# The deep stage's norms on VectorE and ScalarE, its probabilities multiplied on GpSimd, and a new order of the steps

## The chip, the cores and the metric

The kernel runs as one launch on one core of a Trainium2 chip. A core has TensorE (PE, matmuls into PSUM), VectorE (DVE), ScalarE (ACT), GpSimd (POOL) and SyncE (SP, which issues DMAs). Each engine runs its own instructions in order; semaphores tie them together. The metric is the device time of one execution in microseconds. Before the change it is 4638.97 us, the median of three runs (4630.0 to 4643.03).

## The reference

Twelve sublayers are applied in turn to x, four sequences of 512 tokens with 128 channels, each as `x = x + 0.5 * f(layernorm(x))` or without the half: mixture of experts, attentions, channel mixes, SwiGLU, a forget attention, a time mix, and twice the stage of this case, `_L3_ffn_ref`, called "deep":

```python
for i in range(DEPTH):          # 6 layers
    x = attn_layer(shift_tokens(x), Wqkv[i], q_scale[i], k_scale[i], Wo[i]) + x
    x = ffn_layer(shift_tokens(x), ln_g[i], ln_b[i], W1[i], b1[i], W2[i], b2[i]) + x
```

`attn_layer` makes q, k and v of 16 heads of 64, divides each head's q and k by max(norm, 1e-12), multiplies by learned scales and by rotary tables, and attends in windows of 32 tokens to the own and the previous window, with a softmax; its output goes through Wo. `ffn_layer` is a layer norm with gain and offset, a product to twice 341 channels, a times the exact Gelu of the gate, and a product back to 128. All of it is float32.

## The kernel before

x and z lie in SBUF as 128 channels by 2048 tokens, cut into NB = 4 blocks of T = 512. The deep stage works on units: one layer of one block. There are 6 x 4 = 24 units, each of 4 tiles of 128 tokens, so ALL = 96 tiles; the stage runs twice. Each engine's program walks over the steps `s` (`deep_pe`, `deep_act`, `deep_dve`, `deep_pool`), and the order in a step is written out by hand. In step s four tiles are in flight: q and k of tile s are made, tile s-1 is turned, tile s-2 gets its scores and softmax, and tile s-3 its mix with V. `n` is the step's unit and `t` the step in it. The end of unit n-2, its layer norm and feed-forward product, is spread over the four steps (`ending`), and so is Wo of unit n-1 (`begun`).

The work on one tile, with the lines of the profile:

- TensorE multiplies to q, then to k, two matmuls of 512 columns each into PSUM banks 2 and 3 (`qk_pe`, line 1297). ScalarE squares them (1466). VectorE multiplies by the sine and cosine tables (1584, 1588) and sums the squares for each head (1595).
- GpSimd adds the two rotary parts (1703), clamps the sums of squares (1708), raises them to -1/2 (1710) and multiplies q or k with the result (1716). TensorE turns them with eight transposes (1314), ScalarE evicts (1472).
- Scores: eight bf16 matmuls write the mask, 64 small matmuls of 64 rows add q by k (1260, 1266), into banks 0 and 1. V: four products (1328), evicted by ScalarE (1499), moved by SyncE's DMAs.
- Softmax: VectorE takes the maximum (1552), subtracts it (1559), ScalarE does Exp (1476), VectorE sums, inverts (1565, 1567) and multiplies the probabilities (1572). TensorE turns them (1280), ScalarE evicts (1483).
- Mix: 64 small matmuls (1347) into banks 0 and 1 again, evicted as o (1490). Wo: three and five products (1361, 1366).

The end of a unit: mean (1374), centring (1611), squares (1503), variance (1379, 1615), the root as a power on GpSimd (1721), spread over the partitions (1385), scaling (1621), affine (1510), gates (1396), Gelu (1515), a-products (1406), hidden (1630), down product (1412), sum (1636). The banks 4 and 5 hold by turns v, turned q, turned k and turned probabilities, banks 6 and 7 the end of the unit.

Of the kernel before, what the change touches and what calls it, by code (L numbers as in the profile page):

```python
# [19 lines left out]
P = 128  # L20
# [25 lines left out]
def program(nc, d, out, sublayers):  # L46
    with ExitStack() as ctx:
# [25 lines left out]
        minus_half = sb("minus_half", [P, LHEADS])  # L73
# [1079 lines left out]
        def time_dve(dve, u, q, pads):  # L1153
# [19 lines left out]
            for b in range(NB):  # L1173
# [14 lines left out]
                if b >= 1:  # L1188
# [7 lines left out]
                  "deep_sq_summed deep_clamped deep_inv_ready deep_rope_parts deep_summed deep_roped deep_turned deep_turn_kept "  # L1196
# [14 lines left out]
        qT = new(PAIRS, T)  # L1211
# [4 lines left out]
        roped = new(2 * LHEADS, LD)  # L1216
# [5 lines left out]
        h_sum, h_inv = [new(2 * LHEADS) for _ in range(2)], [new(2 * LHEADS) for _ in range(2)]  # L1222
# [26 lines left out]
        def scores_pe(pe, c, j):  # L1249
# [12 lines left out]
            for pair in range(PAIRS):  # L1262
                for jj in range(WPT):
                    for r in range(2):
                        r64, wi = slice(64 * r, 64 * r + 64), WPT * t + jj
                        last = nc.tensor.matmul(bank(r)[32 * jj:32 * jj + 32, pair * 64:pair * 64 + 64],  # L1266
                                                qT[r64, pair, wi * WIN:(wi + 1) * WIN],
                                                kT[r64, pair, wi * WIN:(wi + 2) * WIN], start=False,
                                                stop=(pair == PAIRS - 1), skip_group_check=True)
            last.then_inc(de.deep_scores_ready, 1)  # L1270
# [30 lines left out]
        def turn_pe(pe, c, a, half):  # L1301
            i = c * ALL + a
            pe.wait_ge(de.deep_roped, 2 * i + half + 1)
            if half == 1 and a >= 1:
                pe.wait_ge(de.deep_v_kept, i)
            elif half == 1:
                pe.wait_ge(de.deep_turn_kept, 2 * i + 1)
            elif a >= 2:
                pe.wait_ge(de.deep_probs_kept, i - 1)
            elif a == 1:  # L1310
                pe.wait_ge(de.deep_turn_kept, 2 * i)
            for m in range(PAIRS):
                h = LHEADS * half + 2 * m
                last = nc.tensor.matmul(turns[:, m * P:(m + 1) * P], roped[:, h:h + 2, :], w.ident[:, :], start=True, stop=True,  # L1314
# [3 lines left out]
        def value_pe(pe, c, a):  # L1318
            i, unit_, t = c * ALL + a, a // TILES, a % TILES
            if a + 1 < ALL:  # L1320
                pe.wait_ge(de.deep_turn_kept, 2 * i + 3)
            else:
                pe.wait_ge(de.deep_probs_kept, i)
# [8 lines left out]
        def mix_pe(pe, c, j):  # L1332
# [7 lines left out]
            for pair in range(0, PAIRS, 2):  # L1340
# [9 lines left out]
            last.then_inc(de.deep_pv_done, 1)  # L1350
# [64 lines left out]
        def deep_pe(pe, c):  # L1415
            for s in range(LAST + 1):
                n, t = s // TILES, s % TILES
                ending, begun = 0 <= n - 2 < UNITS, 0 <= n - 1 < UNITS
                if s < ALL:
                    qk_pe(pe, c, s, 0)  # L1420
                if t == 0 and ending:
                    mean_pe(pe, c, n - 2)
                if t == 1 and ending:
                    gate_pe(pe, c, n - 2, 0)
                if 0 <= s - 1 < ALL:
                    turn_pe(pe, c, s - 1, 0)
                if 0 <= s - 2 < ALL:
                    scores_pe(pe, c, s - 2)
                if t == 2 and ending:
                    a_pe(pe, c, n - 2, 2)  # L1430
# [636 lines left out]
```

## Time and profile before

| | |
|---|---|
| median of three runs | 4638.97 us |
| the profiled execution's own time | 4619.88 us |
| its span, first to last instruction | 4618.2 us |
| mean granted clock | 0.964 of full speed |
| busy: TensorE, GpSimd, VectorE, ScalarE | 91%, 67%, 74%, 48% of the span |
| deep stages, from the span's start | about 1067 to 2802 and 2887 to 4612 us |

The trace is one execution. "Busy" is the union of an engine's instructions; matmuls are pipelined and their ends are modelled. A group row gives engine, operation, output and input, count, then busy time, mean ns of one, and the idle time ahead of them with what ended it. PE is the matmul, PEld the weight load. A float32 matmul appears as two records, a transpose as one. "Issue" is time in which the engine waited for nothing that the profile shows.

### The profile page before, as it was taken

What the parts mean: (1) busy time and instruction counts of PE and PEld (TensorE: products, weight loads), DVE (VectorE), ACT (ScalarE), POOL (GpSimd) and SP (SyncE); (2) the same over time, 40 slices, a digit from 0 to 9 for tenths busy, and PEclk for the clock granted to TensorE, in tenths of its full rate; (3) what the DMA queues carried; (4) which work ended last, traced back from release to release, by engine and by line L of the source; (5) the groups of instructions that cost most, each with busy time, mean ns of one, the idle gap of its engine ahead of it and who ended that gap; (6) DMA issues with size and microseconds to landing.
All of it is one profiled execution on the core that took longest, in us unless ns stands there. A gap on an engine that the chain in (4) does not pass through costs nothing.

```text
span 4618.2 us, 148108 instructions
## 1 busy us (share of the span) xinstructions
PE 4211.8 (91%) x66796; PEld 2446.3 (53%) x66796; DVE 3412.0 (74%) x3977; ACT 2202.5 (48%) x2637; POOL 3088.0 (67%) x1726
## 2 busy tenths in 40 slices
PE   7997999867999999999999996799999999999998
PEld 4543433434555555555555553455555555565554
DVE  6567666466777877778778766687788888888885
ACT  1451355323555555555555551355555555555553
POOL 0110000017998898988988960988988988989984
PEclk8998899978999999999999997899999999999999
DMA  2000000001111111111121111111211212121111
GB/s 81 1 2 1 1 1 1 1 0 42 29 32 53 32 31 54 31 53 33 28 56 32 29 32 48 23 32 29 56 29 32 56 29 56 27 57 32 29 32 32
DMA packets 78609, 144.87 MB, mean 31 GB/s; under 512 B 18648, under 2 KB 24992, under 8 KB 76448
## 3 DMA queue, kind: packets, MB, share of 16 engines
q1 hardware_dynamic: 77984, 135.39, 11.5%
q8 instruction: 532, 8.72, 0.8%
q14 instruction: 93, 0.76, 0.1%
HBM read 39.91 MB, written 1.05 MB: 9 GB/s over the span
## 4 chain that ended last, share of the span: by engine, by line
PE 59%; POOL 22%; issue 9%; DVE 8%; ACT 1%; DMA 0%; SPq 0%; POOLq 0%; DVEq 0%
PE psum L1297 9%; POOL arena L1710 8%; POOL arena L1703 6%; POOL arena L1716 5%; PE psum L1314 5%; PE psum L1328 5%; PE psum L666 5%; PE psum L1366 4%; PE psum L1347 4%; PE psum L1266 4%; PE psum L1412 3%; PE psum L1361 3%; PE psum L698 3%; PE psum L720 3%; PE psum L1406 2%
## 5 line engine op out<-in xcount | busy, mean ns | idle before, releaser
L1710 POOL TENSOR_TENSOR arena<-arena,minus_half 128x16 f32<-128x16 f32 x384 | 1129.6, 2942 | 32.0
L1703 POOL TENSOR_TENSOR arena<-arena 128x1024 f32<-128x1024 f32 x384 | 909.2, 2368 | 12.3 <-DVE arena L1588 12.3
L1584 DVE TENSOR_TENSOR arena<-psum,arena 128x1024 f32<-128x1024 f32 x384 | 467.7, 1218 | 399.8 <-ACT arena L1466 399.8
L1716 POOL TENSOR_TENSOR arena<-arena 128x1024 f32<-128x1024 f32 x384 | 733.7, 1911 | 42.6
L1472 ACT ACTIVATE arena<-psum 128x1024 f32<-128x1024 f32 x384 | 392.2, 1021 | 297.5 <-PE psum L1314 297.2
L1466 ACT ACTIVATE arena<-psum 128x1024 f32<-128x1024 f32 x384 | 391.9, 1020 | 253.8 <-PE psum L1297 250.4
L1588 DVE TENSOR_TENSOR arena<-psum,arena 128x1024 f32<-128x1024 f32 x384 | 466.3, 1214 | 54.5 <-PE psum L1314 54.5
L1314 PEld LDWEIGHTS psum<-w_ident,arena 128*128 128x128 f32 x3072 | 354.7, 141 | 279.9 <-issue 151.5
L1499 ACT ACTIVATE arena<-psum 128x1024 f32<-128x1024 f32 x192 | 196.5, 1024 | 580.6 <-PE psum L1328 580.6
L1595 DVE TENSOR_REDUCE arena<-arena 128x16 f32<-128x1024 f32 x384 | 464.4, 1210 | 2.8
L1314 PE MATMUL psum<-w_ident,arena 128*128 128x128 f32 x3072 | 405.6, 275 | 46.3 <-POOL arena L1716 45.4
L1347 PE MATMUL psum<-arena 64*64 64x32 f32 x24576 | 407.2, 220 | 28.6 <-issue 28.5
L1297 PE MATMUL psum<-deep_wqkv,arena 128*128 128x512 f32 x768 | 390.9, 633 | 35.7 <-DVE arena L1588 27.8
L1347 PEld LDWEIGHTS psum<-arena 64*64 64x64 f32 x24576 | 381.8, 135 | 67.4 <-issue 67.3
L1297 PE MATMUL psum<-arena 128*128 128x512 f32 x768 | 372.2, 606 | 0.0
L1266 PE MATMUL psum<-arena 64*32 64x64 f32 x24576 | 296.2, 224 | 66.4 <-issue 66.0
L1266 PEld LDWEIGHTS psum<-arena 64*32 64x32 f32 x24576 | 282.1, 105 | 86.8 <-issue 76.6
L1035 POOL TENSOR_TENSOR arena<-arena 128x512 f32<-128x512 f32 x10 | 14.3, 1450 | 465.8 <-DVE arena L1016 451.7
L1708 POOL TENSOR_SCALAR arena<-arena 128x16 f32<-128x16 f32 x384 | 151.1, 393 | 246.1 <-DVE arena L1595 245.9
L1483 ACT ACTIVATE arena<-psum 128x1024 f32<-128x1024 f32 x192 | 195.6, 1019 | 242.9 <-PE psum L1280 236.8
L1572 DVE TENSOR_TENSOR arena<-arena 128x1024 f32<-128x1024 f32 x192 | 301.7, 1571 | 5.9
L666 PE MATMUL psum<-arena 32*128 32x512 f32 (+3 forms) x1024 | 302.6, 588 | 3.4 <-ACT arena L805 2.3
(264 smaller groups left out, 7277.6 us busy)
## 6 DMA issues: line engine op xcount, KB each, us to landing
arena<-arena SPq DMA_DIRECT2D x672, 128.0 KB, 2.3
deep_wqkv<-in_deep_wqkv SPq DMA_DIRECT2D x6, 1536.0 KB, 7.0
arena<-in_deep_wqkv SPq DMA_DIRECT2D x6, 1536.0 KB, 7.0
arena<-arena SPq DMA_DIRECT2D x96, 64.0 KB, 2.6
deep_wo<-in_deep_wo SPq DMA_DIRECT2D x6, 512.0 KB, 7.3
arena<-in_deep_wo SPq DMA_DIRECT2D x6, 512.0 KB, 7.4
deep_w<-in_deep_w SPq DMA_DIRECT2D x6, 341.0 KB, 7.5
arena<-in_deep_w SPq DMA_DIRECT2D x6, 341.0 KB, 7.4
```

The source lines that it names most:

```text
L666: nc.tensor.matmul(bank(v % SCORE_BANKS)[:, 0:keys], da_Q[r32, b * SETS + s, x_ * P:(x_ + 1) * P], keys_of(causal, b, s)[r32, 0:keys], sta ...
L1266: last = nc.tensor.matmul(bank(r)[32 * jj:32 * jj + 32, pair * 64:pair * 64 + 64], qT[r64, pair, wi * WIN:(wi + 1) * WIN], kT[r64, pair, w ...
L1297: last = nc.tensor.matmul(bank(2 + cc), xs[unit_ % 2][:, WIN + t * P:WIN + (t + 1) * P], wqkv[:, half * INNER + cc * 512:half * INNER + (c ...
L1314: last = nc.tensor.matmul(turns[:, m * P:(m + 1) * P], roped[:, h:h + 2, :], w.ident[:, :], start=True, stop=True, is_transpose=True)
L1347: last = nc.tensor.matmul(bank(odd)[64 * side:64 * side + 64, to:to + WIN], V[64 * r:64 * r + 64, WPT * t + jj, (pair + odd) * 64:(pair + ...
L1472: nc.scalar.activation(dst, turns.rearrange("p (c t) -> p c t", t=P), ACT.Copy).then_inc(de.deep_turn_kept, 1)
L1584: nc.vector.tensor_tensor(turned[:, hs, :].rearrange("p h (a e) -> p h a e", a=2), swapped, sin, ALU.mult).then_inc(de.deep_rope_parts, 1)
L1588: nc.vector.tensor_tensor(roped[:, hs, :], qk_half, under(tabs[:, 2 * half, t, :], shape), ALU.mult).then_inc(de.deep_rope_parts, 1)
L1595: nc.vector.tensor_reduce(h_sum[a % 2][:, hs], qk_sq[:, hs, :], AX.X, ALU.add).then_inc(de.deep_sq_summed, 1)
L1703: nc.gpsimd.tensor_tensor(roped[:, hs, :], roped[:, hs, :], turned[:, hs, :], ALU.add).then_inc(de.deep_summed, 1)
L1710: nc.gpsimd.tensor_tensor(h_inv[a % 2][:, hs], h_inv[a % 2][:, hs], minus_half[:, :], ALU.pow).then_inc(de.deep_inv_ready, 1)
L1716: nc.gpsimd.tensor_tensor(roped[:, hs, :], roped[:, hs, :], over(h_inv[a % 2][:, hs], [P, LHEADS, LD]), ALU.mult).then_inc(de.deep_roped, 1)
```

## The change

**Norms.** VectorE writes the sums of squares of a tile into the first of each pair of `h_pair`, whose second holds the floor 1e-24; a reduce by maximum over the pair is the clamp, a reciprocal over the 32 heads follows (`norms_dve`), and ScalarE takes the Sqrt in the next step (`norms_act`). GpSimd's clamps and powers (`rope_inv_pool`) are gone. GpSimd scales q and k a step later than before; `roped` has two buffers for it, `qT` two tiles instead of a whole block.

**Probabilities.** `divide_dve` becomes `divide_pool`, on GpSimd between the two rotary sums, ahead of the layer norm's root.

**Order.** Scores and mix are each cut into two halves of 64 small float32 products (in pairs of heads), with the value product or the turn of k between. On TensorE the scores go ahead of the turn of q. The mean moves from step 0 to the step 3 before; centring to the start of step 0. On ScalarE the affine step stands behind the Sqrt, and q's eviction behind Exp. The root's spread follows the turn of the probabilities, in transpose mode.

**Copies.** Four VectorE copies of a unit are written as reduces over one element.

```diff
-        minus_half = sb("minus_half", [P, LHEADS])
+        minus_half = sb("minus_half", [P, TILES])
+        h_pair = sb("h_pair", [P, 2 * LHEADS, 2])
...
-        def mix_pe(pe, c, j):
+        def mix_open_pe(pe, c, j):
...
+            mix_pe(j, 0)
+
+        def mix_close_pe(pe, c, j):
+            mix_pe(j, 1).then_inc(de.deep_pv_done, 1)
...
-                                        w.ident[:, :], start=True, stop=True)
+                                        w.ident[:, :], start=True, stop=True, is_transpose=True)
...
                 if s < ALL:
                     qk_pe(pe, c, s, 0)
+                if 0 <= s - 2 < ALL:
+                    scores_open_pe(pe, c, s - 2)
+                    value_pe(pe, c, s - 2)
+                    scores_close_pe(pe, c, s - 2)
                 if t == 0 and ending:
-                    mean_pe(pe, c, n - 2)
+                    var_pe(pe, c, n - 2)
                 if t == 1 and ending:
                     gate_pe(pe, c, n - 2, 0)
+                if t == 2 and ending:
+                    a_pe(pe, c, n - 2, 2)
+                if t == 3 and begun:
+                    wo_rest_pe(pe, c, n - 1)
                 if 0 <= s - 1 < ALL:
                     turn_pe(pe, c, s - 1, 0)
...
                 if s < ALL:
                     qk_pe(pe, c, s, 1)
-                if t == 3 and begun:
-                    wo_rest_pe(pe, c, n - 1)
+                if 0 <= s - 3 < ALL:
+                    mix_open_pe(pe, c, s - 3)
                 if t == 1 and ending:
                     gate_pe(pe, c, n - 2, 1)
                 if 0 <= s - 1 < ALL:
                     turn_pe(pe, c, s - 1, 1)
+                if t == 3 and begun:
+                    mean_pe(pe, c, n - 1)
                 if 0 <= s - 3 < ALL:
-                    mix_pe(pe, c, s - 3)
+                    mix_close_pe(pe, c, s - 3)
...
+        def norms_act(act, c, a):
+            i = c * ALL + a
+            act.wait_ge(de.deep_sq_inv, i + 1)
+            if a >= 2:
+                act.wait_ge(de.deep_roped, 2 * i - 2)
+            nc.scalar.activation(h_inv[a % 2], h_rcp, ACT.Sqrt).then_inc(de.deep_inv_ready, 1)
...
-                if t == 1 and ending:
-                    affine_act(act, c, n - 2)
                 if 0 <= s - 3 < ALL:
                     probs_act(act, c, s - 3)
                 if s < ALL:
                     square_act(act, c, s, 0)
                 if 0 <= s - 1 < ALL:
-                    turn_act(act, c, s - 1, 0)
+                    norms_act(act, c, s - 1)
+                if t == 1 and ending:
+                    affine_act(act, c, n - 2)
                 if t == 0 and ending:
                     ln_square_act(act, c, n - 2)
                 if 0 <= s - 2 < ALL:
                     value_act(act, c, s - 2)
                     exp_act(act, c, s - 2)
+                if 0 <= s - 1 < ALL:
+                    turn_act(act, c, s - 1, 0)
...
+        def norms_dve(dve, c, a):
+            i = c * ALL + a
+            dve.wait_ge(de.deep_sq_summed, 2 * i + 2)
+            nc.vector.tensor_reduce(h_low, h_pair[:, :, :], AX.X, ALU.max).then_inc(de.deep_clamped, 1)
+            dve.wait_ge(de.deep_clamped, i + 1)
+            if a >= 1:
+                dve.wait_ge(de.deep_inv_ready, i)
+            nc.vector.reciprocal(h_rcp, h_low).then_inc(de.deep_sq_inv, 1)
...
-            nc.vector.tensor_copy(xf[0:64, :], zu[0:64, :]).then_inc(de.deep_ffn_shifted, 1)
+            nc.vector.tensor_reduce(xf[0:64, :], single(zu[0:64, :]), AX.X, ALU.max).then_inc(de.deep_ffn_shifted, 1)
...
+        def divide_pool(pool, c, j):
+            i = c * ALL + j
+            pool.wait_ge(de.deep_row_inv, i + 1)
+            nc.gpsimd.tensor_tensor(flat[j % 2], flat[j % 2], over(row_inv, R), ALU.mult).then_inc(de.deep_probs_ready, 1)
...
+                if 0 <= s - 1 < ALL:
+                    rope_scale_pool(pool, c, s - 1, 0)
+                    rope_scale_pool(pool, c, s - 1, 1)
                 if s < ALL:
                     rope_sum_pool(pool, c, s, 0)
+                if 0 <= s - 2 < ALL:
+                    divide_pool(pool, c, s - 2)
                 if t == 0 and 0 <= n - 2 < UNITS:
                     rstd_pool(pool, c, n - 2)
                 if s < ALL:
-                    rope_inv_pool(pool, c, s, 0)
-                    rope_scale_pool(pool, c, s, 0)
-                    rope_inv_pool(pool, c, s, 1)
                     rope_sum_pool(pool, c, s, 1)
-                    rope_scale_pool(pool, c, s, 1)
```

VectorE's order in a step becomes: centring (t = 0), parts of q, maximum and subtraction, sums of q's squares, row sum and reciprocal, the sum of Wo (t = 3), parts of k, sums of k's squares, norms, then scaling (t = 0), the shift of the next unit's input (t = 1, before at t = 2), hidden.

## Rows read from the trace of the kernel before

**Rows 1.** Windows, one in each deep stage: busy us of each engine, clock, DMA.
```profile
core 0: us, PE busy (x) PEld busy (x) DVE busy (x) ACT busy (x) POOL busy (x), PEclk, DMA share, GB/s
1200.00:2700.00 1500.00, 1414.53 (x27106) 866.76 (x27106) 1186.77 (x1198) 802.22 (x838) 1346.82 (x728) 1.00 0.15 38
3000.00:4500.00 1500.00, 1431.40 (x27344) 874.63 (x27345) 1214.29 (x1206) 808.05 (x840) 1354.67 (x731) 1.00 0.15 38
```

**Rows 2.** Timeline of VectorE, the last instruction of two units: start, us.
```profile
1246.53 0.74 DVE L1636 SCALAR_TENSOR_TENSOR z<-psum,deep_vec,z 128x512 f32<-128x512 f32 x1
...
2649.61 0.74 DVE L1636 SCALAR_TENSOR_TENSOR z<-psum,arena,z 128x512 f32<-128x512 f32 x1
```

**Rows 3.** TensorE's waits from 1067 to 4612: us in total, times, longest.
```profile
PE psum L1266 <- issue: 66.0, 67, 1.6
PE psum L1314 <- POOL arena L1716: 45.4, 77, 2.1
PE psum L1385 <- POOL rstd L1721: 36.4, 46, 1.9
PE psum L1347 <- issue: 28.5, 37, 1.6
```

**Rows 4.** Chain of waits inside one unit, pieces in order: start, us, what.
```profile
2001.67 1.72 PE psum L1297 x4
2003.39 0.87 PE psum L1314 x8
2004.27 0.34 PE psum L1260 x8
2004.60 1.28 PE psum L1266 x85
...
2011.58 2.00 PE psum L1347 x128
...
2022.74 1.16 PE psum L1266 x78
2023.90 1.10 issue
...
2025.34 1.89 PE psum L1328 x8
2027.22 1.92 PE psum L1297 x4
2029.14 4.29 PE psum L1366 x10
```

**Rows 5.** Groups by line of the whole span: busy us, mean ns, idle before.
```profile
L1710 POOL TENSOR_TENSOR arena<-arena,minus_half 128x16 f32<-128x16 f32 x384 | 1129.6, 2942 | 32.0
L1703 POOL TENSOR_TENSOR arena<-arena 128x1024 f32<-128x1024 f32 x384 | 909.2, 2368 | 12.3 <-DVE arena L1588 12.3
L1716 POOL TENSOR_TENSOR arena<-arena 128x1024 f32<-128x1024 f32 x384 | 733.7, 1911 | 42.6
L1708 POOL TENSOR_SCALAR arena<-arena 128x16 f32<-128x16 f32 x384 | 151.1, 393 | 246.1 <-DVE arena L1595 245.9
L1721 POOL TENSOR_TENSOR rstd<-arena,minus_half 128x4 f32<-128x4 f32 x48 | 92.2, 1920 | 74.1 <-DVE arena L1615 74.1
L1572 DVE TENSOR_TENSOR arena<-arena 128x1024 f32<-128x1024 f32 x192 | 301.7, 1571 | 5.9
L1559 DVE TENSOR_TENSOR arena<-psum,arena 128x1024 f32<-128x1024 f32 x192 | 234.5, 1221 | 5.1
L1499 ACT ACTIVATE arena<-psum 128x1024 f32<-128x1024 f32 x192 | 196.5, 1024 | 580.6 <-PE psum L1328 580.6
```

**Rows 6.** Timeline of ScalarE where Sqrt is followed by Exp, in the time sublayer.
```profile
2813.07 0.27 ACT L193 ACTIVATE all_std<-psum,eps 128x16 f32<-128x16 f32 x1 [2.64 <-PE psum L172]
2813.36 1.28 ACT L1144 ACT_TABLE_LOAD   x1
2819.87 0.60 ACT L1144 ACTIVATE arena<-psum 128x512 f32<-128x512 f32 x1 [5.22 <-PE psum L1136]
```

More of the change, by code:

```diff
@@ L1210, in program @@
         tabs = new(4, TILES, LD)
-        qT = new(PAIRS, T)
+        qT = [new(PAIRS, P) for _ in range(2)]
         kT = new(PAIRS, WIN + T)
@@ L1215, in program @@
         turned = new(2 * LHEADS, LD)
-        roped = new(2 * LHEADS, LD)
+        roped = [new(2 * LHEADS, LD) for _ in range(2)]
         probs = [new(PAIRS, 2, 2 * WIN) for _ in range(2)]
@@ L1221, in program @@
         xs = [new(WIN + T) for _ in range(2)]
-        h_sum, h_inv = [new(2 * LHEADS) for _ in range(2)], [new(2 * LHEADS) for _ in range(2)]
+        h_low, h_rcp = new(2 * LHEADS), new(2 * LHEADS)
+        h_inv = [new(2 * LHEADS) for _ in range(2)]
         row_max, row_sum, row_inv = (new(LHEADS) for _ in range(3))
@@ L1261, in scores_pe, with scores_close_pe @@
                                      stop=False, skip_group_check=True)
-            for pair in range(PAIRS):
+            scores_pe(j, 0)
+        def scores_close_pe(pe, c, j):
+            scores_pe(j, 1).then_inc(de.deep_scores_ready, 1)
+        def scores_pe(j, part):
+            t = j % TILES
+            for pair in range(PAIRS // 2 * part, PAIRS // 2 * (part + 1)):
                 for jj in range(WPT):
@@ L1303, in turn_pe @@
             pe.wait_ge(de.deep_roped, 2 * i + half + 1)
-            if half == 1 and a >= 1:
+            if half == 1:
+                pe.wait_ge(de.deep_turn_kept, 2 * i + 1)
+            elif a >= 1:
                 pe.wait_ge(de.deep_v_kept, i)
[L1306 to L1311, printed above, removed]
             for m in range(PAIRS):
                 h = LHEADS * half + 2 * m
-                last = nc.tensor.matmul(turns[:, m * P:(m + 1) * P], roped[:, h:h + 2, :], w.ident[:, :], start=True, stop=True,
+                last = nc.tensor.matmul(turns[:, m * P:(m + 1) * P], roped[a % 2][:, h:h + 2, :], w.ident[:, :], start=True, stop=True,
                                         is_transpose=True)
@@ L1339, in mix_pe @@
             apart(pe)
-            for pair in range(0, PAIRS, 2):
+            mix_pe(j, 0)
+        def mix_close_pe(pe, c, j):
+            mix_pe(j, 1).then_inc(de.deep_pv_done, 1)
+        def mix_pe(j, part):
+            t = j % TILES
+            for pair in range(PAIRS // 2 * part, PAIRS // 2 * (part + 1), 2):
                 for jj in range(WPT):
@@ L1349, in mix_pe @@
                                                     probsT[64 * r:64 * r + 64, half, col:col + WIN], start=True, stop=True)
-            last.then_inc(de.deep_pv_done, 1)
+            return last
         WO_FIRST = 3
@@ L1449, in deep_pe @@
                     down_pe(pe, c, n - 2)
-                if t == 0 and ending:
-                    spread_pe(pe, c, n - 2)
                 if t == 2 and begun:
@@ L1455, in deep_pe @@
                     probs_turn_pe(pe, c, s - 2)
+                if t == 0 and ending:
+                    spread_pe(pe, c, n - 2)
                 if t == 1 and ending:
@@ L1654, in deep_dve @@
                 ending, begun = 0 <= n - 2 < UNITS, 0 <= n - 1 < UNITS
+                if t == 0 and ending:
+                    centre_dve(dve, c, n - 2)
+                if t == 2 and ending:
+                    hidden_dve(dve, c, n - 2, 1)
                 if t == 3 and ending:
@@ L1660, in deep_dve @@
                     max_dve(dve, c, s - 2)
[L1661 to L1663 removed]
                     less_max_dve(dve, c, s - 2)
+                if t == 0 and ending:
+                    var_dve(dve, c, n - 2)
                 if s < ALL:
@@ L1683, in deep_dve @@
                 if s < ALL:
+                    parts_dve(dve, c, s, 1)
                     squares_dve(dve, c, s, 1)
-                if t == 3 and begun:
-                    centre_dve(dve, c, n - 1)
+                    norms_dve(dve, c, s)
+                if t == 0 and ending:
+                    scale_dve(dve, c, n - 2)
+                if t == 1 and 2 <= n + 1 < UNITS:
+                    shift_dve(dve, c, n + 1)
                 if t == 1 and ending:
```

78 lines of the change are left out of this document (25 added, 53 removed).

## The prediction

> **What bounds the kernel now.** I read the busy time by windows first, then the clock of the units, then TensorE's waits, then the chain of waits inside one unit. [rows 1] are two stretches of 1500 us, one in each deep stage: TensorE is busy 1414.53 and 1431.40 us (94 and 95%), GpSimd 1346.82 and 1354.67 (90%), VectorE some 80%, ScalarE some 54%, and the granted clock is 1.00, its full level. So the engine to beat is TensorE; GpSimd is a near second. [rows 2] give the period: the instruction that ends a unit (four steps) starts at 1246.53 and, 20 units on, at 2649.61, so 70.15 us for one. TensorE's own time in it, by the mean of the two stretches, is 0.949 x 70.15 = 66.5; its idle time is 3.6.
>
> [rows 3] say what that idle time is. Over both deep stages TensorE waits 66.0 + 28.5 us for "issue", inside the bursts of the scores (line 1266) and of the mix (line 1347), and 45.4 + 36.4 for GpSimd, ahead of the turned q and k (1314) and of the spread root (1385). Over 44 steady units: 94.5 / 44 = 2.1 us of issue in a unit, 81.8 / 44 = 1.9 of GpSimd (a little of it in the first and last units, so that the two give more than 3.6). The reader is to see in [rows 4] how an issue gap looks: the burst of 128 pairs of a weight load and a small matmul runs 1.28 us; the next one breaks off after 78 records for 1.10 us, with no engine to blame. Bursts are the fastest readers of instructions in the stream, so I take the gap for TensorE's instruction stream running dry.
>
> **The change, part by part.** Time zero below is the end of the first qk product of a step.
>
> *GpSimd.* A step had two sums (2368 ns), two scalings (1911), two powers (2942) and two clamps (393) [rows 5]: 15.2 us. The powers and clamps go, the multiplication of the probabilities comes: 128x1024 with a broadcast operand as in the scaling, so 1.91 (at the other end 2.37, a sum's). New: 2 x 2.37 + 3 x 1.91 = 10.5 us, and a root of 1.92 in every fourth step. GpSimd stops being a bound by its sum; only its order can hurt.
>
> *VectorE.* It loses the multiplication (1571 ns, [rows 5]), 6.3 us a unit. It gains per step one reduce over 64 elements and a reciprocal of 32, each at most the 1.22 of a 1024-element instruction and nearer a fourth of it, say 0.6 together, 2.4 a unit; four copies become reduces of 512 elements, between nothing and 0.8 more each, I take 0.7 a unit. Net -3 us on an engine that is idle a fifth of the time: nothing by itself, and its cover is that idle time; were it gone it would still be a gain.
>
> *ScalarE.* A Sqrt of 128x32 a step, 0.27 as the one in [rows 6], and its table. Sqrt, Exp and Gelu alternate, so each step loads twice and one step in four a third time: 9 loads a unit instead of 2. A load is 1.28 us [rows 6]: 7 x 1.28 + 4 x 0.27 = +10 us a unit on an engine that is busy 0.535 x 70.15 = 37.5. The same group shows two things: the load starts 0.02 us after the instruction ahead of it, and it runs before the wait of its own activation, which starts only 5.2 us after the load's end. So a load falls into ScalarE's waiting time where there is any.
>
> *TensorE.* The spread of the root goes into transpose mode: 4 records instead of 8. A turn of eight transposes takes 0.87 [rows 4], so it saves 0.44 a unit. Scores and mix are cut in halves with value, turn or gates between. The half burst of 64 pairs is 0.64 us, then 1.89 us of value product, in which the stream can refill; the gap shown came after 78 records, past the point at which the burst is now cut. I take three quarters of the gaps away, 2.1 to 0.5 a unit; the ends are nothing and all. More changes between small and full tiles cost: a qk product takes 1.92 after the value product and 1.72 after a turn [rows 4], so 0.2 at most per change; three more such changes and one fewer in a step, 0.1 on the average: +0.5 a unit (ends 0 and 1.6).
>
> *What is late next.* With the norms on ScalarE a step later: square 1.02, load 1.28, Sqrt 0.27, some 0.1 of handing over, 2.7; the first scaling 1.91 ends at 4.65, so the turn of q can start at 4.7. TensorE arrives there after masks 0.34, scores 1.28, value 1.89 = 3.5 and the extra of the step. In step 0 that is the variance (eight small matmuls, estimated as 0.87), in 1 a gate and in 2 an a-product (0.86, half of 1.72): 4.4, so 0.3 of waiting in each. In step 3 it is the rest of Wo, 4.29: none. Exp: the value's eviction ends at 4.6, its load at 5.9, and the scores less their maximum are there at 6.0, 2.44 behind the end of value and scores at 3.5 (maximum and subtraction, 1.22 each by [rows 5]); so the load is just covered. Exp (1.05, as an eviction of that size) ends at 7.1, q's eviction at 8.2; TensorE has then done the turn (5.6), qk (7.3) and half the mix (8.3): it just fits. Row sum and reciprocal end at 8.8. GpSimd is at 2.7 + 2 x 1.91 + 2.37 = 8.9 and multiplies to 10.8 (its scaling starts as soon as the root is there). The turn of the probabilities is reached by TensorE at 10.2 in step 0 and later in the other three, which have gates, down product, or Wo between.
>
> In step 0 the root follows: 10.8 + 1.92 = 12.75. TensorE would be at the spread at 4.4 + 0.87 + 1.72 + 2.00 + 0.87 + 0.87 + 0.5 of changes = 11.2. So step 0 waits 1.55 (the 0.3 in it). The unit waits 1.55 + 0.3 + 0.3 = 2.15 for GpSimd, where it waited 1.5 (3.6 - 2.1) for all engines. SyncE's queue keeps its order; its moves of V are released by the value's eviction, which comes no later than before, and the mix that needs them is a step behind: nothing. The affine step now stands behind the Sqrt in ScalarE's order and ends at 3.5, ahead of the gate that needs it (3.5): nothing.
>
> Sum of a unit: 66.5 - 0.44 + 0.5 + 2.15 + 0.5 = 69.2, against 70.15: -0.95. With 44 steady units -42. At the head of a stage some five steps have no layer norm and no feed-forward product: there GpSimd's 15.2 is the bound and the new one is the turn of the probabilities, 10.8 + 0.87 + the next qk, 1.72, so 13.4 and some handing over; I put 4 us a stage, -8 (ends 0 and -20). The drain at the end is a chain that keeps its links: 0. Together -50. The profiled execution is 4619.88 us (span 4618.2 and 1.7 around it), 19 below the median of 4638.97; the difference is put on the median: **4589**, 1.1% faster.
>
> **The rivals.**
>
> *All cover holds.* The small waits of 0.3 and the 1.55 fall in gaps or are absorbed because nothing waits behind them: a unit of 67, 3.1 x 44 = 136 less, so some 4505. For it: the walk takes the later end of each link. Against: the root's chain is strictly serial on one queue.
>
> *The gaps stay.* If the stream runs dry for another reason than the density of the burst, 1.6 a unit come back, less some 0.3 that fall into waits: +57, 4646, within the measurement. For it: by [rows 3] only 67 of 192 score bursts break at all, so density alone does not make a gap. Against: the two lines with bursts hold all of it that matters.
>
> *Slower: ScalarE's order.* In step 1 ScalarE has probabilities, two squares, value, two turns and output (7 x 1.02, [rows 5]), Exp 1.05, three Gelus (2.0), affine 0.8, Sqrt 0.27 and three loads (3.9): 15.2 us of a step of some 16.6. It decides if its waits in order (now 580.6 / 192 = 3.0 us a step before the value alone, [rows 5]) can't be packed into the 1.4 that are left: then step 1 takes 15.2 + 3.0 + 1.0 for its other waits = 19.2, and the other steps 0.5 more, 2.6 + 1.5 = 4.1 a unit, +180: 4769. For it: two thirds busy and in strict order, each eviction holding the same pair of banks. Against: the walk above finds the waits where the loads are.
>
> *Slower: a switch of tables costs twice its load*, because the engine has to fall empty. Another 1.28 in front of Sqrt makes q's turn late by as much in three steps: +3.8 a unit, +169: 4758. [rows 6] speak against it: 0.02 us between the Sqrt and the load. The Trainium skill (ScalarE: Activation LUTs, What ACT_TABLE_LOAD costs) gives 1283 ns for the load and 1380 ns for a drain, 2.66 us a switch, and in Table sets: the hidden batching unit it advises to batch by set, which this change does the opposite of. By its figure the estimate would be 1.38 x 3 a unit, 4.1 x 44 = 182, some 4771. The trace agrees on the load and shows no drain.
>
> **How the numbers follow.** A measurement of this kernel can tell about 0.3% (14 us) from no change. Chances: forecast (4550 to 4622) 0.45, all cover holds 0.17, gaps stay 0.15, ScalarE's order 0.17, double switch 0.03, the change does nothing that matters 0.03. Faster: 0.45 + 0.17 + 0.04 of the third = 0.66. Within: 0.08 of the third, the last and a little of the fourth, 0.13. Slower: 0.21. The range goes from the covered case to the first part of ScalarE's: 4500 to 4680. The likeliest case alone spans 4550 to 4622, by its bounds on gaps and changes.
>
> **What would show it.** TensorE's waits for "issue" at scores and mix fall to a quarter. Its wait at the spread is about 1.2 us a unit, and the turn of q waits 0.3 in three steps of four. ScalarE shows some 430 loads of 1.28 us, busy near 69% in the deep stages. GpSimd falls to about 66% there. A unit takes 69.2. It would be wrong if ScalarE became the releaser of TensorE's long waits, if the GpSimd multiplication took far from 1.9 us, or if the issue gaps stayed at 2 us a unit.

## The result, and the profile after

The changed kernel takes 4494.47 us (median of four runs, 4482.29 to 4501.22), the kernel before 4634.49 beside it: ratio 0.9694, 95% interval 0.9675 to 0.9714, so 140 us less, where 50 were predicted. The profiled execution has a span of 4487.9 us, 130.3 less than before.

The page's first part, busy time by engine:

```profile
PE 4237.0 (94%) x66604; PEld 2403.9 (54%) x66604; DVE 3256.5 (73%) x4169; ACT 2676.0 (60%) x3161; POOL 2128.2 (47%) x1151
```

Windows of the changed kernel, one in each deep stage, as [rows 1]:

```profile
core 0: us, PE busy (x) PEld busy (x) DVE busy (x) ACT busy (x) POOL busy (x), PEclk, DMA share, GB/s
1200.00:2600.00 1400.00, 1394.55 (x26238) 823.07 (x26236) 1096.72 (x1250) 985.51 (x1040) 892.99 (x457) 1.00 0.16 40
2900.00:4300.00 1400.00, 1391.90 (x26371) 825.04 (x26370) 1098.08 (x1252) 986.60 (x1040) 897.40 (x459) 1.00 0.16 40
```

TensorE is busy 99.5% of the two windows, where it had 94 to 95; GpSimd fell from 90% to 64, ScalarE rose from 54 to 70. The ends of two units, as [rows 2]:

```profile
1232.84 0.75 DVE L1669 SCALAR_TENSOR_TENSOR z<-psum,deep_vec,z 128x512 f32<-128x512 f32 x1
...
2577.54 0.75 DVE L1669 SCALAR_TENSOR_TENSOR z<-psum,arena,z 128x512 f32<-128x512 f32 x1
```

A unit takes (2577.54 - 1232.84) / 20 = 67.24 us instead of 70.15. TensorE's waits over both deep stages, as [rows 3] (the window 1067 to 4480; line 1320 is the turn of q and k, 1290 that of the probabilities, 1397 the spread, 1276 and 1359 scores and mix):

```profile
PE psum L1320 <- POOL arena L1739: 15.1, 11, 3.3
PE psum L1290 <- POOL arena L1745: 12.1, 51, 1.5
PE psum L1397 <- POOL rstd L1749: 2.7, 2, 1.3
...
PE psum L1276 <- issue: 0.2, 1, 0.2
```

The 94.5 us of issue are 0.2, the 81.8 us of waiting for GpSimd are 29.9, most of it in the first steps of the stages. The groups of the moved work, as [rows 5]:

```profile
L1739 POOL TENSOR_TENSOR arena<-arena 128x1024 f32<-128x1024 f32 x384 | 722.3, 1902 | 881.8 <-ACT arena L1487 881.8
L1745 POOL TENSOR_TENSOR arena<-arena 128x1024 f32<-128x1024 f32 x192 | 365.3, 1903 | 66.9 <-DVE arena L1592 58.4
L1749 POOL TENSOR_TENSOR rstd<-arena,minus_half 128x4 f32<-128x4 f32 x48 | 48.8, 1016 | 47.5 <-DVE arena L1648 47.5
L1487 ACT ACT_TABLE_LOAD x188 | 241.2, 1283 | 3.3
L1497 ACT ACT_TABLE_LOAD x190 | 243.8, 1283 | 3.3
L1620 DVE TENSOR_REDUCE arena<-h_pair 128x32 f32<-128x64 f32 x192 | 42.2, 220 | 6.7
L1624 DVE RECIPROCAL arena<-arena 128x32 f32<-128x32 f32 x192 | 67.8, 353 | 6.9 <-DVE arena L1620 0.4
```

The multiplication takes 1.90 on GpSimd, the root 1.02 instead of 1.92. ScalarE and GpSimd in a step 0, on the timeline; the qk product ends at 1994.94:

```profile
1994.98 1.03 ACT L1480 ACTIVATE arena<-psum 128x1024 f32<-128x1024 f32 x1 [0.70 <-PE psum L1307]
1996.02 1.28 ACT L1487 ACT_TABLE_LOAD   x1
1997.31 0.23 ACT L1487 ACTIVATE arena<-arena 128x32 f32<-128x32 f32 x1
1997.45 0.62 ACT L1524 ACTIVATE xc_sq<-xc 128x512 f32<-128x512 f32 x1
1997.97 1.00 ACT L1520 ACTIVATE arena<-psum 128x1024 f32<-128x1024 f32 x1
1998.99 1.28 ACT L1497 ACT_TABLE_LOAD   x1
2001.17 1.06 ACT L1497 ACTIVATE arena<-arena 128x1024 f32<-128x1024 f32 x1 [0.89 <-DVE arena L1582]
```
```profile
1997.68 3.76 POOL L1739 TENSOR_TENSOR arena<-arena 128x1024 f32<-128x1024 f32 x2 [3.61 <-ACT arena L1487]
2001.40 2.37 POOL L1733 TENSOR_TENSOR arena<-arena 128x1024 f32<-128x1024 f32 x1
2003.85 1.90 POOL L1745 TENSOR_TENSOR arena<-arena 128x1024 f32<-128x1024 f32 x1
2005.71 1.01 POOL L1749 TENSOR_TENSOR rstd<-arena,minus_half 128x4 f32<-128x4 f32 x1
```

Put the zero at 1994.94: the Sqrt ends at 2.6 (walked: 2.7), GpSimd's multiplication at 10.8 (10.8), the root at 11.8 (12.75). The loads lie in waiting time: the Exp still waits 0.89 for the subtraction behind its load. In the chain of waits of that step TensorE comes to the turn of the probabilities almost with GpSimd:

```profile
1994.94 0.34 PE psum L1262 x8
1995.28 0.66 PE psum L1276 x49
1995.94 1.89 PE psum L1332 x8
1997.83 0.80 PE psum L1276 x53
...
2005.80 1.09 PE psum L1290 x8
2006.90 0.53 PE psum L1397 x4
```

### The profile page after: what moved, and what is told of

The parts are those of the page before. It is cut to its first block, busy times and chain, and to the rows that moved or that the text cites. A ratio compares the mean times of both kernels' runs of the same rounds, so it can differ in the third digit from the quotient of the medians.

```text
span 4487.9 us, 148433 instructions
## 1 busy us (share of the span) xinstructions
PE 4237.0 (94%) x66604; PEld 2403.9 (54%) x66604; DVE 3256.5 (73%) x4169; ACT 2676.0 (60%) x3161; POOL 2128.2 (47%) x1151
## 4 chain that ended last, share of the span: by engine, by line
PE 77%; POOL 8%; issue 7%; DVE 6%; ACT 2%; DMA 0%; SPq 0%; POOLq 0%; DVEq 0%; ACTq 0%
PE psum L1307 13%; PE psum L1359 7%; PE psum L1332 6%; PE psum L1320 6%; PE psum L1276 5%; PE psum L667 5%; PE psum L1378 5%; PE psum L1290 4%; POOL arena L1739 3%; PE psum L1408 3%; PE psum L1424 3%; PE psum L1418 3%; PE psum L1373 3%; PE psum L699 3%; PE psum L721 3%
## 5 line engine op out<-in xcount | busy, mean ns | idle before, releaser
L1739 POOL TENSOR_TENSOR arena<-arena 128x1024 f32<-128x1024 f32 x384 | 722.3, 1902 | 881.8 <-ACT arena L1487 881.8
L1733 POOL TENSOR_TENSOR arena<-arena 128x1024 f32<-128x1024 f32 x384 | 907.5, 2363 | 245.0 <-DVE arena L1608 245.0
L1480 ACT ACTIVATE arena<-psum 128x1024 f32<-128x1024 f32 x384 | 392.4, 1022 | 288.2 <-PE psum L1307 288.2
L1493 ACT ACTIVATE arena<-psum 128x1024 f32<-128x1024 f32 x384 | 390.8, 1018 | 194.6 <-PE psum L1320 194.6
L1615 DVE TENSOR_REDUCE h_pair<-arena 128x16 f32<-128x1024 f32 x384 | 464.2, 1209 | 0.0
L1359 PE MATMUL psum<-arena 64*64 64x32 f32 x24576 | 437.9, 221 | 5.2 <-DVE arena L1582 5.1
L1320 PEld LDWEIGHTS psum<-w_ident,arena 128*128 128x128 f32 x3072 | 338.2, 141 | 162.0 <-POOL arena L1739 94.6
L1745 POOL TENSOR_TENSOR arena<-arena 128x1024 f32<-128x1024 f32 x192 | 365.3, 1903 | 66.9 <-DVE arena L1592 58.4
L1504 ACT ACTIVATE arena<-psum 128x1024 f32<-128x1024 f32 x192 | 196.7, 1024 | 257.9 <-PE psum L1290 251.6
L1276 PE MATMUL psum<-arena 64*32 64x64 f32 x24576 | 327.2, 223 | 0.3 <-issue 0.2
L667 PE MATMUL psum<-arena 32*128 32x512 f32 (+3 forms) x1024 | 303.6, 590 | 3.4 <-ACT arena L806 2.3
L1497 ACT ACTIVATE arena<-arena 128x1024 f32<-128x1024 f32 x192 | 202.9, 1057 | 173.8 <-DVE arena L1582 173.8
L699 PE MATMUL psum<-arena 32*128 32x512 f32 (+3 forms) x1024 | 293.3, 558 | 1.8 <-ACT arena L831 1.8
L1575 DVE TENSOR_REDUCE arena<-psum 128x16 f32<-128x1024 f32 x192 | 235.2, 1225 | 61.1 <-PE psum L1276 61.1
L831 ACT ACTIVATE arena<-psum 128x512 f32<-128x512 f32 (+3 forms) x344 | 161.0, 514 | 170.8 <-PE psum L699 169.4
```

Of the source, the lines that this page charges most:

```text
L667: nc.tensor.matmul(bank(v % SCORE_BANKS)[:, 0:keys], da_Q[r32, b * SETS + s, x_ * P:(x_ + 1) * P], keys_of(causal, b, s)[r32, 0:keys], sta ...
L699: nc.tensor.matmul(bank(key_at[m])[:, q0:T], kk[r32, kt * P:(kt + 1) * P], da_Q[r32, b * SETS + s, q0:T], start=True, stop=True).then_inc( ...
L1320: last = nc.tensor.matmul(turns[:, m * P:(m + 1) * P], roped[a % 2][:, h:h + 2, :], w.ident[:, :], start=True, stop=True, is_transpose=True)
L1359: last = nc.tensor.matmul(bank(odd)[64 * side:64 * side + 64, to:to + WIN], V[64 * r:64 * r + 64, WPT * t + jj, (pair + odd) * 64:(pair + ...
L1480: nc.scalar.activation(qk_sq[:, HALVES[half], :], qk_half, ACT.Square).then_inc(de.deep_qk_squared, 1)
L1615: nc.vector.tensor_reduce(h_pair[:, hs, 0], qk_sq[:, hs, :], AX.X, ALU.add).then_inc(de.deep_sq_summed, 1)
```

## The experiments

All are timed against the kernel before on their own chip; ratios to it in brackets. Waits are of the window 1250 to 2450, some 17 units of the first deep stage. A half is 32 float32 products, which are 64 records in the profile (the section on the change calls it 64 products).

**Halves alone, on the kernel before.**

```diff
-                    scores_pe(pe, c, s - 2)
...
-                    value_pe(pe, c, s - 2)
+                    scores_open_pe(pe, c, s - 2)
+                    value_pe(pe, c, s - 2)
+                    scores_close_pe(pe, c, s - 2)
...
+                if 0 <= s - 3 < ALL:
+                    mix_open_pe(pe, c, s - 3)
                 if 0 <= s - 1 < ALL:
                     turn_pe(pe, c, s - 1, 1)
                 if 0 <= s - 3 < ALL:
-                    mix_pe(pe, c, s - 3)
+                    mix_close_pe(pe, c, s - 3)
```


> The kernel before with the one edit that scores and mix are cut in halves of 64 pairs, the value product between the halves of the scores and the turn of k between those of the mix; norms, GpSimd and all other orders as before. Theory A (the issue gaps come from dense bursts that read the instruction stream dry): TensorE's waits for issue at scores and mix fall from 94.5 us to under 10, and the time by 50 to 80 us, to 4555 to 4585. Theory B (GpSimd's 15 us a step is a bound just behind TensorE, and the gaps only fill its time): the issue waits fall too, but TensorE's waits for GpSimd grow from 82 us by about as much, and the time stays within 20 us of 4634. Theory C (the gaps have another cause, such as the data transfers): issue stays near 95 us and so does the time.

Measured 4701.87 us (1.0147, 1.0126 to 1.0168): 66 slower. Its waits:

```profile
PE psum L1399 <- POOL rstd L1737: 22.7, 17, 1.3
PE psum L1321 <- POOL arena L1732: 11.6, 17, 0.7
PE psum L1410 <- ACT arena L1531: 9.8, 17, 0.6
PE psum L1361 <- DVE arena L1575: 9.1, 16, 0.6
PE psum L1335 <- ACT arena L1488: 4.6, 29, 0.2
```

No issue is left in the window (in the second stage 5.1 us, at the mix), so the halves end nearly all gaps; no theory had the rest. In the old order the value product needs q evicted, now sits inside the scores and holds their second half up; maximum, subtraction, root and mix follow later. These waits only take the place of the gaps, though: over 20 units from 1318.76 to 2745.90 TensorE is idle 3.9 us a unit, as before. What is added is its own busy time, 67.50 us a unit instead of 66.12 (12.4 us more at the mix and 10.3 at the scores in the 20), which I put down to more changes between small and full tiles.

**GpSimd relieved, on the kernel before.**

```diff
-            nc.gpsimd.tensor_tensor(h_inv[a % 2][:, hs], h_inv[a % 2][:, hs], minus_half[:, :], ALU.pow)
+            nc.gpsimd.tensor_tensor(h_inv[a % 2][:, hs], h_inv[a % 2][:, hs], minus_half[:, :], ALU.mult)
```

> The kernel before with GpSimd's power of 128x16 replaced by a product of the same shape, so that GpSimd is relieved of most of 2 x 2.94 us a step (the inverse root of the norms is left out); all orders as before. Theory A and B both: TensorE's waits for GpSimd (82 us) go. Theory A: the issue gaps of 94.5 us stay, and the time falls by 60 to 80 us, to about 4565. Theory B: with GpSimd out of the way the gaps are all that is left, and the time falls by less than 50 us, since what waited for GpSimd now meets the gaps.

Measured 4516.76 (0.9742, 0.9728 to 0.9757): 119 less, more than expected. GpSimd's waits are down to the spread, and in the first stage the gaps stay:

```profile
PE psum L1266 <- issue: 36.2, 35, 3.0
PE psum L1385 <- POOL rstd L1721: 4.4, 18, 0.3
PE psum L1347 <- issue: 3.7, 8, 0.7
```

In the second stage they nearly go, with the same code, whole bursts and full clock. These are 20 units of each stage, and the waits of the second 20:

```profile
1310.67:2679.78 1369.11, 1319.54 (x25358) 810.81 (x25355) 1109.56 (x1120) 747.76 (x780) 803.29 (x678) 1.00 0.16 39
3098.34:4425.70 1327.36, 1311.74 (x25361) 809.22 (x25361) 1110.57 (x1119) 749.34 (x780) 803.50 (x678) 1.00 0.16 41
```
```profile
PE psum L1266 <- issue: 5.3, 15, 0.5
PE psum L1347 <- issue: 5.0, 13, 1.0
```

So the gaps at the bursts are 2.2 us a unit in one stage and 0.5 in the other, and dense bursts alone do not make them; what differs between the stages is open. The unit there takes 66.37 us, less than the changed kernel's 67.24.

**Both of them.** The two edits together.

> Both edits of the two kernels above at once on the kernel before (the inverse root of the norms is left out). If the two causes are all of the change, this comes to the changed kernel's 4494 us within 20, with TensorE busy 98% or more of the deep stages. If the new order of scores ahead of the turn of q, or the probabilities on GpSimd, bring something of their own, it stays 40 us or more above. If the causes add up, its gain is the sum of the two single gains within 15 us; if each hides the other (theory B), it is more than the sum by 30 us or more.

Measured 4684.72 (1.0101, 1.0081 to 1.0121). With GpSimd out of the way the halves cost 168 us in the old order. The gains do not add; in this order the halves are a loss.

**Whole bursts, on the changed kernel.**

```diff
-                    value_pe(pe, c, s - 2)
                     scores_close_pe(pe, c, s - 2)
+                    value_pe(pe, c, s - 2)
...
-                if 0 <= s - 3 < ALL:
-                    mix_open_pe(pe, c, s - 3)
...
                 if 0 <= s - 1 < ALL:
                     turn_pe(pe, c, s - 1, 1)
...
+                    mix_open_pe(pe, c, s - 3)
                     mix_close_pe(pe, c, s - 3)
```


> The changed kernel with scores and mix as whole bursts again (value behind the scores, turn of k ahead of the mix), the rest as changed. Theory A: the issue gaps come back with 80 to 100 us, and the time rises by 60 to 90 us, to about 4570. If the gaps were made by anything but the density of the bursts, issue stays near 0 and the time rises by less than 15 us; it may even fall by up to 25 us, if the changes between tile sizes cost what was predicted (0.5 us a unit).

Measured 4621.41 (0.9976, 0.9959 to 0.9993): 127 slower than the changed kernel, and close to the kernel before. The trace is of an execution of 4637.41 us. Its window and waits:

```profile
1250.00:2450.00 1200.00, 1134.91 (x21515) 677.50 (x21512) 898.75 (x1028) 811.95 (x856) 736.64 (x380) 0.99 0.16 40
```
```profile
PE psum L1359 <- issue: 24.9, 26, 4.2
PE psum L1320 <- ACT arena L1492: 16.7, 34, 0.5
PE psum L1276 <- issue: 12.6, 19, 1.1
PE psum L1320 <- ACT arena L1519: 5.6, 26, 0.2
```

Issue comes back at 37.5 / 17.1 = 2.2 us a unit, but 1.3 more are waits of the turns for ScalarE: for the evictions of q (line 1492) and of v (1519). The value product stands later, and behind it hang its eviction, the table load, Exp and q's eviction. The halves pay twice.

**Only the scores whole; only the mix whole.** The two parts of that edit, one at a time.

> The changed kernel with the scores as one burst ahead of the value product; the mix stays in halves. Theory D (the halves pay twice: the instruction stream keeps up, and the value product comes 0.7 us earlier for ScalarE's chain of value, table load, Exp, q's eviction, turn of k): issue gaps of 0.7 to 1.2 us a unit come back at the scores alone, none at the mix, and TensorE waits some 0.5 us a unit for ScalarE ahead of the turn of k; 4530 to 4560. Theory A alone (only the stream): issue gaps as said, no wait for ScalarE; 4525 to 4540.

> The changed kernel with the mix as one burst behind the turn of k; the scores stay in halves. Theory D: issue gaps come back at the mix alone, 0.7 to 1.5 us a unit; and the turn of k, now 1.0 us earlier in the order, waits for q's eviction some 0.5 us in two of four steps; 4540 to 4580. Theory A alone: 4525 to 4545 and no wait for ScalarE. If neither gap nor wait shows, the mix's halves were worth nothing and the run is 10 to 25 us faster than the changed kernel, for two fewer changes of tile size a step.

Measured 4489.74 (0.9696, 0.9670 to 0.9722) for the scores: equal to the changed kernel, against both theories. Issue is 5.1 us in 18 units, the turns wait 8.8 for GpSimd and 1.9 for ScalarE, and TensorE's saved changes pay for that: its busy time is 66.36 us a unit instead of 66.97. The mix: 4560.95 (0.9849, 0.9824 to 0.9873), 66 slower:

```profile
PE psum L1320 <- ACT arena L1492: 29.0, 39, 0.8
PE psum L1359 <- issue: 6.9, 9, 1.1
PE psum L1276 <- issue: 2.6, 4, 1.2
```

So the mix's halves do the work, by covering q's eviction ahead of the turn of k (1.7 us a unit) more than by the gaps (0.6). With one burst whole the gaps are 0.3 to 0.6 us a unit and with both 2.2, and the costs, -5 and 66 us, add up to half of the 127: why is open.

**One more table load a step.**

```diff
+            nc.scalar.activation(sqrt_first[:, 2:3], eps[:, :], ACT.Sigmoid)
             nc.scalar.activation(h_inv[a % 2], h_rcp, ACT.Sqrt).then_inc(de.deep_inv_ready, 1)
```

> The changed kernel with one more table load a step: a Sigmoid on a scratch column ahead of the Sqrt, which loads its own table (1.28 us, and about 0.2 for the column). It stands for a switch that costs twice. If GpSimd's start is the tight link, as the prediction's walk has it (q's turn can start at 4.7, TensorE arrives at 4.4 to 4.6), the 1.5 us go onto three steps of four and onto the root in step 0: 4 to 5 us a unit, 180 to 220 us, 4680 to 4710. If ScalarE has slack there that the walk did not see, it is under 60 us.

Measured 4714.24 (1.0182, 1.0160 to 1.0204): 220 more than the changed kernel; a unit of the first stage takes 71.85 us, 4.6 more, as the walk's tight link says.

```profile
PE psum L1320 <- POOL arena L1740: 35.9, 50, 1.5
PE psum L1408 <- ACT xc L1532: 20.1, 17, 1.2
PE psum L1391 <- ACT xc_sq L1525: 17.2, 17, 1.0
```

A late Sqrt holds up q's turn, and the gate and the variance, which wait for the affine step and the squares behind it. That the loads which the change adds cost next to nothing is read from the changed kernel's small waits, and not from a run without them.

**GpSimd's powers back, as idle work.** `burn_pool` is a power of two scratch tiles.

```diff
                     rope_scale_pool(pool, c, s - 1, 0)
+                    burn_pool(pool)
                     rope_scale_pool(pool, c, s - 1, 1)
+                    burn_pool(pool)
```

> The changed kernel with GpSimd's two powers of 128x16 a step put back as work on a scratch tile, one behind each scaling; nothing uses them. GpSimd then has 10.5 + 5.9 = 16.4 us a step, near the step of 16.8. If GpSimd's relief is what makes the new order possible, the multiplication of the probabilities ends 5.9 us later and TensorE waits in every step: 150 to 400 us more. If the order alone makes the gain, it stays within 60 us of 4494.

Measured 5220.18 (1.1268, 1.1245 to 1.1292): 726 more, beyond the range. The turn of the probabilities waits 136.8 us in the window for GpSimd, and the granted clock is 0.93 there instead of 1.00. A unit of the first stage takes 82.09 us: of the 14.9 more, 11.1 are TensorE idle and 3.8 its own slower work. GpSimd is busy only 80% of it, so it is its place in the chain that costs, and not its sum.

**The spread without transpose mode; copies instead of reduces; the root ahead of the probabilities; the multiplication on VectorE.**

```diff
-                                        w.ident[:, :], start=True, stop=True, is_transpose=True)
+                                        w.ident[:, :], start=True, stop=True)
```
```diff
-            nc.vector.tensor_reduce(xf[0:64, :], single(zu[0:64, :]), AX.X, ALU.max).then_inc(de.deep_ffn_shifted, 1)
+            nc.vector.tensor_copy(xf[0:64, :], zu[0:64, :]).then_inc(de.deep_ffn_shifted, 1)
...
```
```diff
-                if 0 <= s - 2 < ALL:
-                    divide_pool(pool, c, s - 2)
                 if t == 0 and 0 <= n - 2 < UNITS:
                     rstd_pool(pool, c, n - 2)
+                if 0 <= s - 2 < ALL:
+                    divide_pool(pool, c, s - 2)
```
```diff
-                    divide_pool(pool, c, s - 2)
...
+                    divide_dve(dve, c, s - 2)
                 if t == 3 and begun:
                     attn_dve(dve, c, n - 1)
```

> The changed kernel with the root's spread as a plain float32 product (8 records instead of 4). By the prediction's term it costs 0.44 us a unit, 20 us. If TensorE is the only bound now (99.6% busy), all of it shows: 4505 to 4520. If step 0 still waits for GpSimd elsewhere, less than 10 us show.

> The changed kernel with the four reduces over one element a unit written as copies again. VectorE wins 4 x 0.2 us a unit and has slack, so nothing is won there. Theory: copies held GpSimd up (the clamp before took 393 ns in the mean and 250 in most), now GpSimd has slack too: within 15 us of 4494. Rival: a GpSimd instruction in the tight link behind the Sqrt is held up by copies, 0.3 to 1 us a unit: 15 to 45 us more.

> The changed kernel with the layer norm's root ahead of the multiplication of the probabilities in GpSimd's order in step 0. The turn of the probabilities stands ahead of the spread on TensorE and then waits for the root's length more. If the root takes 1.0 us as in the changed kernel: 1.0 us a unit, 40 to 50 us. The root took 1.92 in the kernel before, where it stood right behind a sum; here it does again. If its length goes by the instruction ahead of it, it is 1.9 to 2.0 again and the cost 80 to 95 us.

> The changed kernel with the multiplication of the probabilities back on VectorE, right behind the reciprocal, before the sum of Wo and the parts of k; norms stay on VectorE and ScalarE. The probabilities are then ready at 10.1 instead of 10.8 in step 0, but the parts of k and the norms come 1.3 us later and the next qk product waits for the former: they end at 12.9 where TensorE is at 11.9 in step 0 and later elsewhere. I expect 0.5 to 1.2 us a unit more: 4515 to 4550. If VectorE's slack takes it, the run is equal to the changed kernel, or up to 15 us faster by the 0.3 us of waiting in step 0, and the move to GpSimd was worth nothing.

| | us | ratio (95%) | against the changed kernel |
|---|---|---|---|
| spread as a plain product | 4519.82 | 0.9754 (0.9738 to 0.9771) | +25 |
| copies | 4490.83 | 0.9693 (0.9667 to 0.9719) | equal |
| root first | 4527.75 | 0.9768 (0.9750 to 0.9785) | +33 |
| multiplication on VectorE | 4513.93 | 0.9738 (0.9716 to 0.9761) | +19 |

The first shows whole, as on an engine that is the only bound. The root first cost less than the 40 to 50 us expected. The root took 1.02 in all four, right behind a sum too: its length does not go by the instruction ahead. The multiplication's move is worth some 19 us, the intervals being just apart (0.9714 and 0.9716); TensorE then waits hardly more (0.34 us idle a unit instead of 0.27), but is busy 67.13 us a unit instead of 66.97, and why was not followed.

**An earlier Sqrt, alone and with whole scores; a clamp on GpSimd.** The last is a `tensor_scalar` of 128x16 on a scratch tile behind the second scaling.

```diff
+                if 0 <= s - 1 < ALL:
+                    norms_act(act, c, s - 1)
                 if s < ALL:
                     square_act(act, c, s, 0)
-                if 0 <= s - 1 < ALL:
-                    norms_act(act, c, s - 1)
```

> The changed kernel with the Sqrt of the norms and its table load ahead of the square of q in ScalarE's order, where ScalarE idles for 1.2 to 1.6 us. GpSimd starts its scaling 1.2 to 1.5 us earlier after the qk product. If the tight link is this chain, TensorE's 0.2 us of waiting a unit for GpSimd goes and the first steps of a stage, which wait 1.05 + 0.18 us each for GpSimd, get 1.2 us shorter: 10 to 20 us less, 4474 to 4484. If the load now delays the square of q and with it the parts and the maximum, which step 0 can't cover: 5 to 20 us more.

> The early Sqrt together with whole score bursts. Whole bursts alone gave 4489.74 us: they save a change of tile size a step but made TensorE wait 0.5 us a unit for GpSimd ahead of the turn of q, 0.1 for ScalarE and 0.3 for issue. With the early Sqrt the 0.5 goes: 15 to 30 us less than the changed kernel, 4465 to 4480. If issue gaps take what is freed (they were 2.2 us a unit with both bursts whole), it stays above 4480.

> The changed kernel with one clamp of 128x16 (a tensor_scalar, on a scratch tile that nothing uses) behind the second scaling of each step on GpSimd. If the root's 1.92 us came from clamps in the instruction mix, it is about 2.0 us again, and the time rises by 1.0 for the root and 0.3 for the clamp in step 0: 40 to 70 us. If not, the root stays at 1.02 and only the clamp's 0.3 to 0.4 us show in step 0: 10 to 20 us.

Measured 4491.81 (0.9696, 0.9673 to 0.9719), 4502.8 (0.9717, 0.9702 to 0.9731) and 4494.35 (0.9709, 0.9688 to 0.9729). None beats the changed kernel. The first and the last show neither the gain nor the cost expected; the second stays above 4480, but with gaps of only 0.3 us a unit. With the earlier Sqrt the waits only move, to 6.4 us for q's eviction and 7.1 for the probabilities: the square of q is later. A clamp does not bring the long root back, and its own 0.25 us do not show.

## Why the prediction was wrong

The direction held, and so did the walk of the new step on ScalarE and GpSimd. The size did not: 4494 lies 6 us under the range. Nor did the account of where the gain comes from: the prediction had the waits for GpSimd grow from 1.5 to 2.15 us a unit, and all of the gain in the gaps, the spread and the stages' heads. The rival that all cover holds had put 67 us a unit and 4505, and came nearest.

- *The waits for GpSimd, 2.15 us a unit, are the step that failed.* The window 1250 to 2450 has 3.5 us of them in 17.8 units, 0.2 a unit. Of the 1.95 between, 0.9 is the root (1.02, not 1.92). The rest is TensorE's own path, which I walked too short: masks, scores and value take 3.69 and not 3.51, since the two changes of tile size fall in there, and a gate or an a-product behind the scores takes 1.02 to 1.06 and not 0.86. 4.7 is just when GpSimd lets q's turn start. I had charged the changes to the unit, and the waits beside them, when the one fills the other.
- *The gaps*: predicted down to 0.5, now none in 20 units. Size off by 0.5. The cause, dense bursts, is not shown: the halves end nearly all gaps in both orders, but whole bursts have few in one stage of the kernel with GpSimd relieved. There the rival that density alone does not make a gap was right.
- *TensorE's own time*: predicted 66.56, now 0.996 x 67.24 = 66.97; 0.4 the other way. The spread's term of 0.44 measured 25 us / 48 = 0.53. The changes of tile size, put at 0.5, are then 66.97 + 0.53 less the 66.1 to 66.4 of before (the table below): 1.1 to 1.4, near the upper end that was given.
- *The sum*: 69.2 was predicted, 67.24 came. Over the 20 + 20 units between the marks the trace is 58.4 + 48.2 us shorter, where 40 x 0.95 = 38 were expected. (The second stage had a unit of 69.65 before, so its gain is smaller.)
- *The head of a stage*: the first unit ends 13.7 and 13.2 us earlier, predicted 4 each. The new step was walked right: its qk products start at 1124.33 and 1137.99, 13.66 apart, against 13.4 "and some handing over". I had counted too few steps and put too little on each. The drain is 3 us longer.
- *ScalarE's order, and the double switch*: neither came. Busy 70% (69 said), and a load starts with the instruction before it and holds none up. The extra load shows how near it was, as far as one more load stands for a switch that costs twice: 1.5 us more, and the change would have been 80 us slower than the kernel before.
- *VectorE* at nothing was right for the copies; the norms took 0.57 us a step (0.6 said) and were not tried apart; that the multiplication's move is worth 19 us was not in it.

What made the gain is seen in units, each the mean of 20 from the end of a stage's second unit on, with TensorE's busy and idle time in them:

| | first stage: unit, busy, idle (us) | second stage: unit, busy, idle (us) |
|---|---|---|
| before | 70.03, 66.12, 3.91 | 69.50, 66.42, 3.08 |
| halves alone, old order | 71.36, 67.50, 3.86 | 71.49, 67.60, 3.89 |
| relief alone, old order | 68.46, 65.98, 2.48 | 66.37, 65.59, 0.78 |
| both, old order | 70.55, 67.32, 3.23 | 70.65, 67.44, 3.22 |
| changed | 67.24, 66.97, 0.27 | 67.25, 66.97, 0.27 |
| changed, whole bursts | 70.24, 66.32, 3.92 | 70.58, 66.64, 3.93 |
| changed, scores whole | 67.40, 66.36, 1.04 | 67.45, 66.40, 1.04 |
| changed, mix whole | 68.53, 66.34, 2.20 | 68.46, 66.30, 2.15 |

Relieving GpSimd alone gives 119 us in the old order. The new order with the relief but whole bursts gives 14. The halves give it 127 more, 21 beyond the relief alone. That each piece has another worth in another order is shown. The halves buy idle time off with busy time (0.6 us a unit for either burst alone and 0.65 for both in the new order, 1.4 in the old); relief alone, where its gaps are few, has the shorter unit. A version of the old order with the real norms was not run.

## What to carry to other kernels

Where one engine is near full, walk its own path with every penalty at its place before charging a wait: a cost on that path and a wait behind it are not added, the larger counts. Cutting a burst has a price in TensorE's own time, and pays only where what moves ahead of or between the halves covers a wait of another engine's chain; in the old order it lost 66 us. Read a gap in every stage before giving it a cause. Table loads were free here up to the length of the wait in front of them, and after that one cost in full.

## What the runs showed of the hardware

- TensorE's gaps for issue inside bursts of 128 pairs (0.5 to 2.6 us a unit with both bursts whole, by stage and kernel) are all but gone with bursts of 64 and slower products between (0 to 0.3).
- The Exp's load runs ahead of its activation's wait (0.89 us of waiting left behind it above).
- GpSimd's power of 128x4 takes 2.00 to 2.06 us in most units of the kernels with the old norms and 1.02 to 1.04 on average in all with the new ones; neither the instruction ahead, nor a clamp nearby, nor a power of 128x16 a step (1.015 there) makes the difference. In the kernel before 44 of 48 roots started while VectorE's multiplication (line 1572) ran, and all took 2.00 to 2.03. Four were short: two at the ends of the stages, with VectorE idle, and two (at 3452.79 and 4008.47) where the sum ahead of the root started just behind that multiplication and took 3.35 and 3.39 us instead of 2.37. So the extra 1.0 us fell on the GpSimd instruction that started while that multiplication ran, the root or not. With the multiplication back on VectorE in the new order the root started 0.03 us ahead of it and took 1.02. No run was made for this; why is open.

```profile
3449.29 1.32 DVE L1572 TENSOR_TENSOR arena<-arena 128x1024 f32<-128x1024 f32 x1
```
```profile
3449.48 3.35 POOL L1703 TENSOR_TENSOR arena<-arena 128x1024 f32<-128x1024 f32 x1
3452.79 1.02 POOL L1721 TENSOR_TENSOR rstd<-arena,minus_half 128x4 f32<-128x4 f32 x1
```

- The same multiplication on VectorE, two SBUF operands, took 1571 ns on average in the kernel before (1226 in the median, up to 3391), 1635 with GpSimd's powers left out, and 1226 in the new order; so the powers did not lengthen it.
- With TensorE waiting more, in the run with idle powers, the mean granted clock fell to 0.93 in the window of the first deep stage and 0.91 in one of the second, between its two levels of 1.2 and 2.4 GHz.
